# A layer's four-tap filter of v taken as four accumulated matmul products instead of vector operations

## The reference, cut to what matters

```
def _causal_dwconv(x, w):
    xc = jnp.moveaxis(x, 1, 2)
    y = jax.lax.conv_general_dilated(xc, w, window_strides=(1,), padding=[(w.shape[-1] - 1, 0)], ...,
                                     feature_group_count=w.shape[0])
    return jnp.moveaxis(jax.nn.silu(y), 1, 2)
...
q = _causal_dwconv(x @ Wq, conv_q).reshape(Bx, Lx, NH, HD)
k = _causal_dwconv(x @ Wk, conv_k).reshape(Bx, Lx, NH, HD)
v = _causal_dwconv(x @ Wv, conv_v).reshape(Bx, Lx, NH, HD)
q = q / jnp.linalg.norm(q, axis=-1, keepdims=True)
k = k / jnp.linalg.norm(k, axis=-1, keepdims=True)
```

## Time and profile before

| | |
|---|---|
| median of 3 runs | 1680.47 us (1678.34 to 1684.89) |
| the profiled execution's own time | 1683.24 us |
| its span, first to last instruction | 1681.5 us |
| the delta layer in it | from about 1264.3 us to 1464.1 us |
| the twelve filters on DVE in it | 1276.45 us to 1309.99 us |

### The profile page before, as it was taken

The page is one execution under the profiler, slowest core; times in us unless marked ns, Lnnn a source line. Parts: engine busy times, 40 slices in busy tenths (PEclk is TensorE's granted clock), DMA queues, the critical chain, the costliest instruction groups (busy, mean ns, idle before and its releaser), DMA issues. The chain is left out here.

```text
span 1681.5 us, 26802 instructions
## 1 busy us (share of the span) xinstructions
PE 1382.7 (82%) x9088; PEld 941.8 (56%) x9088; DVE 1180.0 (70%) x2866; ACT 774.6 (46%) x1412; POOL 731.4 (43%) x921
## 2 busy tenths in 40 slices
PE   4699999956996539997799898899994588389998
PEld 3333333244884327873477676677872377276886
DVE  5877777456556674558799898697778644769776
ACT  2277777730222221216887664545554311064654
POOL 3833332025642017620088787066672141006665
PEclk9699999968997869998899999999997699589999
DMA  1244240000100000100011110564530000164543
GB/s 39 65 116 130 77 139 24 2 26 13 38 26 12 0 26 26 38 13 19 22 45 41 35 45 20 214 134 123 134 105 7 0 1 1 25 216 120 139 131 106
DMA packets 77883, 104.76 MB, mean 62 GB/s; under 512 B 25185, under 2 KB 43121, under 8 KB 77233
## 3 DMA queue, kind: packets, MB, share of 16 engines
q1 hardware_dynamic: 77760, 103.23, 21.7%
HBM read 92.81 MB, written 10.39 MB: 61 GB/s over the span
## 5 line engine op out<-in xcount | busy, mean ns | idle before, releaser
L526 DVE CUSTOM_DVE_ANT_1 la_neg<-bank,la_table 128x512 f32<-128x512 f32 x256 | 166.4, 688 | 41.5 <-PE bank L617 40.8
L1699 POOL TENSOR_TENSOR lh_h_low<-lh_hidden,lh_h_high 128x512 fp32r<-128x512 f32 x84 | 111.3, 1327 | 161.9 <-ACT lh_h_high L1732 161.6
L1412 DVE TENSOR_TENSOR_SCAN le_h<-le_keep,bank 128x512 f32<-128x512 f32 x128 | 152.2, 1209 | 24.0 <-issue 19.6
L1497 PEld LDWEIGHTS bank<-le_diag,le_dtxT 128*128 128x128 f32 x1024 | 125.6, 191 | 57.8 <-issue 41.7
L1699 POOL TENSOR_TENSOR lf_h_low<-lf_hidden,lf_h_high 128x512 fp32r<-128x512 f32 x84 | 111.1, 1325 | 106.6 <-ACT lf_h_high L1732 106.3
L1497 PE MATMUL bank<-le_diag,le_dtxT 128*128 128x128 f32 x1024 | 132.4, 277 | 21.2 <-DVE le_h L1412 13.6
L453 ACT ACTIVATE la_probT<-bank 128x512 f32<-128x512 f32 x256 | 135.6, 605 | 11.4 <-PE bank L636 9.3
L1722 ACT ACTIVATE bank<-bank 128x512 f32<-128x512 f32 x144 | 83.7, 582 | 62.0 <-PE bank L1887 60.3
L1345 ACT ACTIVATE le_keep<-le_dt,le_A 128x512 f32<-128x512 f32 x128 | 87.1, 711 | 17.5 <-DVE le_h L1412 17.5
L1255 POOL TENSOR_TENSOR le_hc<-le_h,le_c_row 128x512 f32<-128x512 f32 x64 | 81.4, 1272 | 30.0 <-issue 20.5
L48 PE MATMUL bank<-ident 128*128 128x512 bf16 x142 | 45.2, 489 | 59.0 <-DVEq L830 40.4
(11 more groups left out here) (570 smaller groups left out, 3611.7 us busy)
## 6 DMA issues: line engine op xcount, KB each, us to landing
lf_weight<-lf_scratch SPq DMA_DIRECT2D x128, 128.0 KB, 3.0
lh_weight<-lh_scratch SPq DMA_DIRECT2D x128, 128.0 KB, 3.2
le_c_row<-le_scratch SPq DMA_DIRECT2D x32, 256.0 KB, 3.1
la_table<-la_scratch SPq DMA_DIRECT2D x4, 1792.0 KB, 7.0
lf_weight<-lf_scratch SPq DMA_DIRECT2D x64, 64.0 KB, 2.2
lh_weight<-lh_scratch SPq DMA_DIRECT2D x64, 64.0 KB, 2.2
la_bias_parts<-la_scratch_parts SPq DMA_DIRECT2D x12, 248.0 KB, 6.2
lb_w1s<-in_L_ffn_w_dram SPq DMA_DIRECT2D x8, 256.0 KB, 2.8
```

What stands on the lines that cost most here:

```text
L526: dve.tensor_tensor_reduce(out=neg[:, u % 2, :].rearrange("p (c i) -> p c i", i=P), in0=k.bank[u % RING1][:].rearrange("p (c i) -> p c i", ...
L1412: dve.tensor_tensor_scan(h[:, i, :], keep[:, i, :], k.bank[4 + q % 2][:], 0.0, ALU.mult, ALU.add).then_inc(scanned, 1)
L1497: last = pe.matmul(k.bank[4 + q % 2][:, j * P:(j + 1) * P], dtxT[:, (g * G2 + bb) * TPB + j, c, :], diag[:, d % DIAGS, j, :], start=True, ...
L1699: pool.tensor_tensor(h_low[:, u % RING, :], hidden[:, u % RING, :], h_high[:, u % RING, :].bitcast(F32), ALU.subtract)\
```

## The change

Only v is changed. Ahead of the layer norm's transposes, PE now waits for the weights and turns Wv into bank 4; ACT scales the turned matrix by each of the four taps (`wv_turned`, one tap weight per partition); PE turns the four results back into bank 5; ACT copies them to `wv_taps`. A projection of v is then four products that add up in one bank: the tap for "now" over all 512 columns, and the three earlier ones with output shifted right by 1, 2 and 3 columns. ACT takes silu of v straight from the bank into `s3` (semaphore `v_ready`), so that v has no copy to `xp` and no filter on DVE. q and k go as before.

```
         @block.scalar
         def _(act):
             norm.scalar_sqrt(act)
+            act.wait_ge(loaded_w, 16 * NW)
+            act.wait_ge(wv_first, 1)
+            for j in range(TAPS):
+                act.activation(wv_turned[:, j, :], k.bank[4][:, 0:D], ACT.Copy, scale=cw[:, 2, j:j + 1]).then_inc(wv_scaled, 1)
+            act.wait_ge(wv_second, 1)
+            act.activation(wv_taps[:].rearrange("p j d -> p (j d)"), k.bank[5][:], ACT.Copy).then_inc(wv_ready, 1)
             norm.scalar_copy(act)
...
-                for i in range(3):
-                    act.wait_ge(conv_ready, b * 3 + i + 1)
+                for i in range(2):
+                    act.wait_ge(conv_ready, b * 2 + i + 1)
                     act.activation(s3[:, i, b, :], s3[:, i, b, :], ACT.Silu).then_inc(act_ready, 1)
...
                     act.wait_ge(in_done, n + 1)
-                    act.activation(xp[:, i, b, TAPS - 1:], k.bank[4 + n % 4][:], ACT.Copy).then_inc(in_copied, 1)
+                    if i == 2:
+                        act.activation(s3[:, i, b, :], k.bank[4 + n % 4][:], ACT.Silu).then_inc(v_ready, 1)
+                    else:
+                        act.activation(xp[:, i, b, TAPS - 1:], k.bank[4 + n % 4][:], ACT.Copy).then_inc(in_copied, 1)
...
             for b in range(B):
-                for i in range(3):
-                    dve.wait_ge(in_copied, b * 3 + i + 1)
+                for i in range(2):
+                    dve.wait_ge(in_copied, b * 2 + i + 1)
...
         @block.tensor
         def _(pe):
+            pe.wait_ge(loaded_w, 16 * NW)
+            pe.transpose(k.bank[4][:, 0:D], w3[:, 2, :], k.ident[:]).then_inc(wv_first, 1)
+            pe.wait_ge(wv_scaled, TAPS)
+            for j in range(TAPS):
+                last = pe.transpose(k.bank[5][:, j * D:(j + 1) * D], wv_turned[:, j, :], k.ident[:])
+            last.then_inc(wv_second, 1)
             norm.tensor(pe)
-            pe.wait_ge(loaded_w, 16 * NW)
+            pe.wait_ge(wv_ready, 1)
...
-                    pe.matmul(k.bank[4 + n % 4][:], w3[:, i, :], k.xnT[:, b * T:(b + 1) * T], start=True, stop=True).then_inc(in_done, 1)
+                    bank = k.bank[4 + n % 4]
+                    if i < 2:
+                        pe.matmul(bank[:], w3[:, i, :], k.xnT[:, b * T:(b + 1) * T], start=True, stop=True).then_inc(in_done, 1)
+                    else:
+                        for back in range(TAPS):
+                            last = pe.matmul(bank[:, back:T], wv_taps[:, TAPS - 1 - back, :], k.xnT[:, b * T:(b + 1) * T - back],
+                                             start=(back == 0), stop=(back == TAPS - 1))
+                        last.then_inc(in_done, 1)
```

More of the change, by code:

```diff
@@ L2007, in layer_delta @@
         ones = sb("ones", [P, P])
+        wv_turned = sb("wv_turned", [P, TAPS, D])
+        wv_taps = sb("wv_taps", [D, TAPS, D])
         ident2 = sb("ident2", [P, P])
@@ L2031, in layer_delta @@
         order, pool_order = sem("order"), sem("pool_order")
+        wv_first, wv_scaled, wv_second, wv_ready, v_ready = sem("wv_first"), sem("wv_scaled"), sem("wv_second"), sem("wv_ready"), sem("v_ready")
         in_done, in_copied, conv_ready, act_ready = sem("in_done"), sem("in_copied"), sem("conv_ready"), sem("act_ready")
@@ L2100, in _ @@
             norm.scalar_sqrt(act)
+            act.wait_ge(loaded_w, 16 * NW)
[4 more added lines that the diff above has]
+            act.activation(wv_taps[:].rearrange("p j d -> p (j d)"), k.bank[5][:], ACT.Copy).then_inc(wv_ready, 1)
             norm.scalar_copy(act)
             def silu_and_squares(b):
-                for i in range(3):
-                    act.wait_ge(conv_ready, b * 3 + i + 1)
+                for i in range(2):
+                    act.wait_ge(conv_ready, b * 2 + i + 1)
                     act.activation(s3[:, i, b, :], s3[:, i, b, :], ACT.Silu).then_inc(act_ready, 1)
                 for i, squares in enumerate((sq, sq_k)):
-                    act.wait_ge(act_ready, b * 3 + i + 1)
+                    act.wait_ge(act_ready, b * 2 + i + 1)
                     act.activation(squares[:, b, :], s3[:, i, b, :], ACT.Square).then_inc(sq_ready, 1)
@@ L2159, in _ @@
                     last.then_inc(conv_ready, 1)
-            dve.wait_ge(act_ready, 3 * B)
+            dve.wait_ge(act_ready, 2 * B)
+            dve.wait_ge(v_ready, B)
             for i in range(2):
@@ L2251, in _ @@
                     if n >= 4:
-                        pe.wait_ge(in_copied, n - 3)
-                    pe.matmul(k.bank[4 + n % 4][:], w3[:, i, :], k.xnT[:, b * T:(b + 1) * T], start=True, stop=True).then_inc(in_done, 1)
+                        bb, ii = (n - 4) // 3, (n - 4) % 3
+                        if ii == 2:
+                            pe.wait_ge(v_ready, bb + 1)
+                        else:
+                            pe.wait_ge(in_copied, bb * 2 + ii + 1)
+                    bank = k.bank[4 + n % 4]
+                    if i < 2:
+                        pe.matmul(bank[:], w3[:, i, :], k.xnT[:, b * T:(b + 1) * T], start=True, stop=True).then_inc(in_done, 1)
+                    else:
+                        for back in range(TAPS):
+                            last = pe.matmul(bank[:, back:T], wv_taps[:, TAPS - 1 - back, :], k.xnT[:, b * T:(b + 1) * T - back],
+                                             start=(back == 0), stop=(back == TAPS - 1))
+                        last.then_inc(in_done, 1)
             pe.wait_ge(wbr_ready, 1)
@@ L2257, in _ @@
             pe.wait_ge(pool_order, 2 + 3 + 1 + B)
-            pe.wait_ge(in_copied, 3 * B)
+            pe.wait_ge(in_copied, 2 * B)
+            pe.wait_ge(v_ready, B)
             pe.wait_ge(beta_ready, B)
```

## The result

The change is faster, by 0.46%, a little less than the 0.5% that the prediction names as what a measurement of this kernel can tell from no change: a median of 1677.83 us over 19 runs against 1684.89 us for the kernel before over 19 runs beside them, ratio 0.9954, 95% interval 0.9939 to 0.997, which leaves out 1. The forecast was 1674.4, or a ratio of 0.9964 (1674.4 / 1680.47); it lies inside the interval. One disturbed run of 2762 us is left out of the ratio.

A forecast was written before the change was run, and what follows sets the result against it. DVE bounds the stretch from 1276 to 1310 us. Removing 11.0 us of filters and 0.36 of slow first operation, against 3.6 late start, 1.1 wait and 0.7 clock, gains 6.0 us: 1674.4 us, range 1670 to 1680.5.

The forecast's parts named there:

- DVE's filters are the bound: Delta layer, 1276 to 1310 us: DVE never waits between the twelve filters, and what follows hangs on the last.
- Removed, 11.0 and 0.36 us: DVE's filters: four filters of 2.76 us go, 11.0 us, plus 0.36 us of a slow first operation.
- The preparation, 3.6 us: Ahead of the filters: waiting for all transfers, transposes and scalings make the first product 3.6 us late.
- The new wait, 1.1 us: Ahead of DVE's fifth filter: q2's copy stands behind ACT's silus and squares, so DVE waits 1.1 us.
- PE keeps ahead, 0.86 us a product: Beside the filters: six products take PE 5.2 us per sequence against DVE's 5.5, shifted products costing 0.86 like others.
- The clock, 0.7 us: First products after the transposes: a possibly low PE clock adds 0.7 us, between no and two late products.
- the second of the other ways: First products: clock low through q0, k0 and part of v0; gain 4 to 5 us, time 1676, chance 0.20.
- The sum, 6.0 us: End of the last filter: all gains and costs together bring it 6.0 us earlier.
- The cheaper way: Preparation: clock rises early in the transposes and no new ACT wait; gain 8.9 us, time 1671.6, chance 0.13.

The follow-up runs named there:

- preparation alone: Kernel before plus only the change's weight preparation on PE and ACT, prepared weights unused and v's filters kept on DVE: ratio 1.0026.
- root first: The change with Wv and taps loaded first, earlier scalings, previous sequence's silus and squares before v's silu, one-column root as ACT's first instruction: ratio 0.9935.
- two products more: The change with two extra, overwritten products ahead of each v's four: filters end at 43.88 us from the layer's first row, one run.
- the same with PE kept busy: The root first kernel with eleven useless products on PE while it waits for weights and scalings: ratio 0.9945.
- the best layer alone: The root first kernel cut to its delta layer, other seven layers left out: 202.15 us over 4 runs.
- early load: The change with Wv and its taps loaded first on their own semaphore and the scalings ahead of the layer norm's root: ratio 0.9948.
- both: The change with early load, and with the previous sequence's silus and squares ahead of v's silu on ACT: ratio 0.9955.
- the layer alone: Delta layer only, other seven layers left out: kernel before 212.7 us, the change 205.19, the root first version 202.15.

## Why the prediction was right, step by step

- *DVE's filters are the bound.* Shown: where they end earlier or later by 3.8 us or more, the layer does too, by 8.1 us for 6.25 (the change), 4.6 later for 3.8 (preparation alone), 11.9 for 10.4 (root first). The tail is 8.0 to 8.1 us long as before, but for the run with two products more (9.15).
- *Removed, 11.0 and 0.36 us.* Shown: eight filters 2.76 us apart, and the first operation takes 0.48. That POOL was the reason for 0.84 is likely, not shown: the operation took 0.48 or 0.49 wherever POOL had ended its set-up, and 0.61, 0.52 and 0.49 in the three other executions where it had not (root first, the same with PE kept busy, and the best layer alone).
- *The preparation, 3.6 us.* The first product came at 13.95 us from the layer's first row; forecast was 1278.3 - 1264.36 = 13.94. By its steps: the weights 7.86 (forecast 7.64), from the first transpose to the second burst 1.77 (1.8), and twenty transposes 4.32 (4.4). These forecasts add up to 13.84, the prediction wrote 0.1 us more, and the errors cancel: that it fits to 0.01 us is luck, that each step fits to 0.2 us is not. The experiment with the preparation alone shows that it is paid.
- *The new wait, 1.1 us.* The mechanism and the place were right, the size was 0.80: without the 0.6 us of clock, the copy was done 13.7 us after the first product and not 13.9, as the count let ACT's instructions follow each other a little too slowly, and DVE came free at 12.9 and not 12.8. With ACT's order altered the wait is gone, which shows the cause.
- *PE keeps ahead, 0.86 us a product.* Shown: 5.14 us per sequence. From the first record of v to the next row are 3.42 us for eight records, six of them shifted (1285.88 to 1289.30), and 1.72 us for four of q and k (1289.30 to 1291.02). Both are 0.43 us per record, so the shift costs nothing.
- *The clock, 0.7 us.* It was low in the first pair: 2.50 instead of 1.88, 0.62 us. The 0.7 was a middle between none and two late products that no row gave, so its size is luck. What came is the mild end of what I had set apart as the second of the other ways; the Trainium skill's rule on transposes, cited there ("TensorE: Matmul & The Clock Gate", Part 4, PE-mode transpose), fits this execution, where the clock rose only after four records of products, but not that of before.
- *The sum, 6.0 us.* 6.25 at the end of the filters. The whole kernel shows 7.1 us between medians with an interval of 5.1 to 10.3 (0.3% and 0.61% of 1684.89); the 0.8 us beyond 6.25 cannot be told from nothing.

The cheaper way was not taken by the change, but it is there: with the weights loaded first, the table load kept at the start and ACT's order altered, 10.4 of the 11 us arrive. This is the best version that was run (1673.89 us beside 1683.94, ratio 0.9935); its interval overlaps the change's, so in the whole kernel it is not shown to beat it, in the layer alone it is (201.65 to 202.99 against 203.51 to 205.47).

## What to carry to other kernels

When work is moved off the engine that bounds a stage, ask what the new preparation waits for: a semaphore that counts all transfers makes the first user wait for the last and least urgent of them. Then follow each in-order engine past the moved instruction; here a silu that waits for eight products held back a copy behind it. And an instruction put first on ACT can move a table load from idle time onto the path.

## What the runs showed of the hardware that was not expected

- Products into a bank at an offset of 1 to 3 columns, adding to what is there, run at the same 0.43 us per record as others.
- The same sixteen transposes were followed by the high clock in the kernel before and by the low clock in the changed kernel, where they ended a row of twenty that had run at 0.50. The kernels "early load" and "both" have the same instructions on PE up to there, and the first pair took 1.88 us in one execution and 2.97 in the other. So what the first products cost after such a stage differs from one execution to the next; in the change's it was 0.6 us.
- One stretch at the low clock in the products of `wT` and `uT` made 1.6 us of difference between two executions whose work there is the same.
